# The second batch's normalised rows, turned by way of DRAM and VectorE instead of on TensorE

## The reference

```python
def _layernorm(x, axis=-1, eps=1e-05):
    m = jnp.mean(x, axis=axis, keepdims=True)
    v = jnp.var(x, axis=axis, keepdims=True)
    return (x - m) / jnp.sqrt(v + eps)
...
# attention: x is (2, 512, 512), 32 heads of 16
def proj(w):
    y = jnp.einsum('bsd,ed->bse', x, w)
    return y.reshape(B, S, HEADS, D_K).transpose(0, 2, 1, 3)
q, k, v = (proj(w_q), proj(w_k), proj(w_v))
scores = jnp.einsum('bhqd,bhkd->bhqk', q, k) / jnp.sqrt(jnp.float32(D_K))
attn = jax.nn.softmax(scores, axis=-1)
out = jnp.einsum('bhqk,bhkd->bhqd', attn, v)
...
# ffn: 8 experts, 800 wide, the two best for each token
h1 = jnp.einsum('th,efh->tef', xt, w1)
h3 = jnp.einsum('th,efh->tef', xt, w3)
act = jax.nn.silu(h1) * h3
expert_out = jnp.einsum('tef,ehf->teh', act, w2)
y = jnp.einsum('te,teh->th', w_full, expert_out)
...
x = x + _L0_attn_ref(_layernorm(x, axis=-1), ...)
x = x + _L0_ffn_ref(_layernorm(x, axis=-1), ...)
```

## Time and profile before

| | |
|---|---|
| device time, median of 3 runs | 544.2 us (543.85 to 544.46) |
| the profiled execution: its own time | 544.47 us |
| the profiled execution: span | 542.7 us |
| PE busy | 528.0 us, 97% of the span |
| DVE busy | 386.5 us, 71% |
| ACT busy | 321.2 us, 59% |
| mean granted TensorE clock | 0.994 of full speed |

### The profile page before, as it was taken

One profiled execution on the slowest core, in us unless ns is written; L12 is line 12 of the kernel. 1 busy time (PEld: TensorE's weight loads), 2 busy tenths in 40 slices (PEclk: granted clock), 3 DMA queues, 4 the chain that ended last, 5 costly groups with the idle time before them and its releaser, 6 DMA issues.

```text
span 542.7 us, 10567 instructions
## 1 busy us (share of the span) xinstructions
PE 528.0 (97%) x3925; PEld 388.4 (72%) x3925; DVE 386.5 (71%) x722; ACT 321.2 (59%) x476; POOL 116.9 (22%) x146
## 2 busy tenths in 40 slices
PE   7999999999999999999999999999999999999992
PEld 6887665343333434334868989999999999999991
DVE  6924766999998999943979986836648284666650
ACT  4422115888778788777373465746576575757540
POOL 3400111001020220722001320432342321242112
PEclk9999999999999999999999999999999999999997
DMA  8381267675685470033645698774846757585122
GB/s 298 148 104 14 42 110 84 103 95 79 97 104 74 72 159 15 14 101 99 240 159 170 225 372 266 198 259 111 312 80 220 223 154 269 124 297 162 40 36 38
DMA packets 29743, 78.24 MB, mean 144 GB/s; under 512 B 8572, under 2 KB 9596, under 8 KB 25210
## 3 DMA queue, kind: packets, MB, share of 16 engines
q1 hardware_dynamic: 24394, 68.84, 47.1%
q0 software_dynamic: 5296, 8.69, 8.6%
HBM read 53.11 MB, written 9.32 MB: 115 GB/s over the span
## 4 chain that ended last, share of the span: by engine, by line
PE 89%; DVE 5%; DMA 1%; issue 1%; POOL 1%; ACT 1%; SPq 0%; POOLq 0%; DVEq 0%
PE ps L719 17%; PE ps L721 16%; PE ps L720 16%; PE ps_o L734 12%; PE ps L747 7%; PE ps L759 5%; PE ps_m L747 3%; DVE neg_max L1458 3%; PE ps L787 2%; PE ps_o L719 1%; PE ps_m L1016 1%; DMA x_sb<-x 1%; PE ps L1068 1%; PE ps L1071 1%; PE ps_o L720 1%
## 5 line engine op out<-in xcount | busy, mean ns | idle before, releaser
L1241 ACT ACTIVATE probs_t<-ps 128x1024 f32<-128x1024 f32 x128 | 125.7, 1023 | 28.1 <-PE ps_o L734 23.6
L1458 DVE TENSOR_REDUCE neg_max<-ps 128x1 fp32r<-128x512 f32 x171 | 111.2, 681 | 7.2 <-PE ps L747 4.5
L719 PE MATMUL ps<-xgT_hi,w_hi 128*128 128x256 f32 (+7 forms) x380 | 109.4, 288 | 0.0
L721 PE MATMUL ps<-xgT_hi,w_lo 128*128 128x256 f32 (+7 forms) x380 | 108.6, 286 | 0.0
L720 PE MATMUL ps<-xgT_lo,w_hi 128*128 128x256 f32 (+7 forms) x380 | 108.5, 286 | 0.0
L759 PE MATMUL ps<-q_stack,k_stack 49*128 49x512 f32 x256 | 83.8, 444 | 0.0
L734 PE MATMUL ps_o<-probs_t,v_ones 128*32 128x256 f32 (+1 forms) x944 | 79.6, 409 | 0.1
L719 PEld LDWEIGHTS ps<-xgT_hi,w_hi 128*128 128x128 f32 x380 | 72.0, 189 | 0.3 <-DVE xgT_lo L1733 0.2
L720 PEld LDWEIGHTS ps<-xgT_lo,w_hi 128*128 128x128 f32 x380 | 72.0, 190 | 0.1
L721 PEld LDWEIGHTS ps<-xgT_hi,w_lo 128*128 128x128 f32 x380 | 72.0, 189 | 0.0
L747 PE MATMUL ps<-k_stack,q_stack 48*128 48x512 f32 x171 | 68.6, 458 | 0.5 <-DVE neg_max L1458 0.5
(11 more groups left out here) (326 smaller groups left out, 981.6 us busy)
## 6 DMA issues: line engine op xcount, KB each, us to landing
w_sb<-w SPq DMA_DIRECT2D x16, 1024.0 KB, 7.2
w_sb<-w SPq DMA_DIRECT2D x8, 1536.0 KB
w_sb<-w SPq DMA_DIRECT2D x8, 1152.0 KB, 8.3
q_stack<-q_hi SPq DMA_DIRECT2D x32, 128.0 KB, 4.8
k_stack<-k_hi SPq DMA_DIRECT2D x32, 128.0 KB, 4.6
q_stack<-q_lo SPq DMA_DIRECT2D x16, 128.0 KB, 4.4
k_stack<-k_lo SPq DMA_DIRECT2D x16, 128.0 KB, 5.7
q_hi<-o_raw SPq DMA_DIRECT2D x16, 128.0 KB, 4.8
```

The lines of the kernel that those rows point to most:

```text
L719: pe.matmul(o, x_hi, w_hi, start=start, stop=False)
L721: return pe.matmul(o, x_lo, w_hi, start=False, stop=stop)
L1241: a.activation(probs_t[:, kc % 2, 2 * half:2 * half + 2, :], ps4[:, 2 * (n % 2):2 * (n % 2) + 2, :], ACT.Exp, scale=D ** -0.5).then_inc(s_ ...
L1458: v.tensor_reduce(neg_max[:, g % 2, col:col + 1], max_bank(g, u2), AX.X, ALU.max, negate=True).then_inc(s_mx, 1)
```

## The change

The sixteen transposes of batch 1 leave PE. In their place:

1. SP waits until all 8 tiles are normalised (`s_xn`), writes the four tiles of batch 1 to a DRAM tensor `xn_rows` in one transfer of 1 MB, waits for it (`s_xw`), and reads it back in four transfers of 256 KB. Read n takes columns 128n to 128n+127 of every row to partitions 32n to 32n+31, in pieces of 512 bytes. All five stand in SP's queue ahead of `ready(0)` and `stack(0)`.
2. DVE, at job ("t", 1, 0), waits for the four reads (`s_xr`) and turns the four tiles in 32x32 blocks, in place.
3. ACT and DVE then make `xnT_hi` and `xnT_lo` of batch 1 from `x_sb` in SBUF, with a step of four elements, instead of from PSUM.
4. Block turning puts hidden index 4p + c on partition p in chunk c. So the weights of q, k and v are laid out in this order by the host, in the same sizes, and the transposes of batch 0, which stay on PE, read `x_sb` with a step of four elements.

```diff
+    xn_dram = nc.dram_tensor("xn_rows", [S, HID], f32, kind="Internal").ap()
...
+        s_xw, s_xr, s_xd1 = sem("s_xw"), sem("s_xr"), sem("s_xd1")
...
+        on_pe = [j[:2] != ("t", 1) for j in jobs]
+        j_count = [sum(on_pe[:n + 1]) for n in range(len(jobs))]
...
+        def x_turned(n):
+
+            _, b, i = jobs[n]
+            if b:
+                return x_sb[:, TPB + i, :].rearrange("p (t c) -> p c t", c=HC)
+            return job_bank[n].rearrange("p (c t) -> p c t", c=HC)
...
             sp.dma_start(xn2_dram[0:1, :], rec_row[0:1, :]).then_inc(s_rows, 16)
+
+            sp.wait_ge(s_xn, NT)
+            sp.dma_start(xn_dram[:, :].rearrange("(n p) h -> p n h", p=P), x_sb[:, TPB:NT, :]).then_inc(s_xw, 16)
+            sp.wait_ge(s_xw, 16)
+            pieces = x_sb[:, TPB:NT, :].rearrange("p n (g k) -> p (n g) k", k=P)
+            for n in range(P // BLOCK):
+                sp.dma_start(pieces[BLOCK * n:BLOCK * (n + 1), :, :],
+                             xn_dram[:, n * P:(n + 1) * P].rearrange("(m j) k -> j m k", j=BLOCK)).then_inc(s_xr, 16)
...
-                        last = pe.transpose(o[:, c * P:(c + 1) * P], x_sb[:, b * TPB + i, c * P:(c + 1) * P], ident[:, :])
+                if on_pe[n]:
+                    before = [m for m in range(n) if on_pe[m] and bank_of[m] == bank_of[n]]
...
+                            last = pe.transpose(o[:, c * P:(c + 1) * P],
+                                                x_sb[:, i, :].rearrange("r (p c) -> r c p", c=HC)[:, c, :], ident[:, :])
...
-                a.wait_ge(s_job, n + 1)
+                a.wait_ge(s_job, j_count[n])
                 if kind == "t":
-                    a.activation(xnT_hi[:, :, i * P:(i + 1) * P], o.rearrange("p (c t) -> p c t", c=HC),
-                                 ACT.Copy).then_inc(s_ja, 1)
+                    if not on_pe[n]:
+                        a.wait_ge(s_xd1, i + 1)
+                    a.activation(xnT_hi[:, :, i * P:(i + 1) * P], x_turned(n), ACT.Copy).then_inc(s_ja, 1)
...
                 if kind == "t":
+                    if (b, i) == (1, 0):
+                        v.wait_ge(s_xr, 16 * (P // BLOCK))
+                        for t in range(TPB, NT):
+                            blocks = x_sb[:, t, :].rearrange("p (g k c) -> p g c k", k=BLOCK, c=HC)
+                            v.transpose(blocks, blocks).then_inc(s_xd1, 1)
                     v.wait_ge(s_ja, a_count[n])
                     at = slice(i * P, (i + 1) * P)
-                    v.tensor_tensor(xnT_lo[:, :, at], job_bank[n].rearrange("p (c t) -> p c t", c=HC),
-                                    xnT_hi[:, :, at].bitcast(f32), ALU.subtract).then_inc(s_jd, 1)
+                    v.tensor_tensor(xnT_lo[:, :, at], x_turned(n), xnT_hi[:, :, at].bitcast(f32),
+                                    ALU.subtract).then_inc(s_jd, 1)
...
-        "wq": rows_first(np.asarray(L0_attn_w_q).T[:, order]),
+        "wq": fours_first(np.asarray(L0_attn_w_q).T[:, order]),
```

More of the change, by code:

```diff
@@ L625, in _ @@
                                base=0, pattern=[[1, E], [-1, E]], channel_multiplier=0).then_inc(s_const, 1)
-            pool.wait_ge(s_job, n_of["q", 1, HC - 1] + 1)
+            pool.wait_ge(s_job, j_count[n_of["q", 1, HC - 1]])
             prepare(1)
-            pool.wait_ge(s_job, n_of["k", 1, HC - 1] + 1)
+            pool.wait_ge(s_job, j_count[n_of["k", 1, HC - 1]])
             prepare(2)
-            pool.wait_ge(s_job, len(jobs))
+            pool.wait_ge(s_job, j_count[-1])
             prepare(3)
@@ L806, in _ @@
                     keep_warm(job_bank[NB - 1], 6)
[L807 to L813, removed]
-                        last = pe.transpose(o[:, c * P:(c + 1) * P], x_sb[:, b * TPB + i, c * P:(c + 1) * P], ident[:, :])
[L815 to L820, removed]
-                    else:
[L822 to L828, removed]
-                        else:
-                            last = three(o, *(t[:, at] for t in w2), *x2, c == 0, c == HC - 1)
@@ L831, in _ @@
-                last.then_inc(s_job, 1)
+                if on_pe[n]:
+                    before = [m for m in range(n) if on_pe[m] and bank_of[m] == bank_of[n]]
+                    if before:
+                        job_read(pe, before[-1])
+                    o = job_bank[n]
+                    if kind == "t":
+                        pe.wait_ge(s_xn, b * TPB + i + 1)
+                        for c in range(HC):
+                            last = pe.transpose(o[:, c * P:(c + 1) * P],
+                                                x_sb[:, i, :].rearrange("r (p c) -> r c p", c=HC)[:, c, :], ident[:, :])
+                    else:
+                        which = "qkv".index(kind)
+                        at = slice(i * P, (i + 1) * P)
+                        opening = kind == "q" and (b, i) in ((0, 0), (0, 1), (1, 0))
+                        if opening:
+                            last = opened(o, at, b, i)
+                        else:
+                            pe.wait_ge(s_wl, which + 1)
+                            pe.wait_ge(s_jd, d_count[n_of[("t", b, TPB - 1)]])
+                        for c in range(0 if opening else HC):
+                            x2 = [t[:, c, :] for t in (xnT_hi, xnT_lo)]
+                            w2 = [t[which][:, c, :] for t in (w_hi, w_lo)]
+                            if kind == "v":
+                                last = three(o, *(t[:, at] for t in x2), *w2, c == 0, c == HC - 1)
+                            else:
+                                last = three(o, *(t[:, at] for t in w2), *x2, c == 0, c == HC - 1)
+                    last.then_inc(s_job, 1)
@@ L1227, in _ @@
                 if (s, p) == (0, 1):
-                    a.wait_ge(s_job, len(jobs))
+                    a.wait_ge(s_job, j_count[-1])
                     a.activation(v_ones[:, NT - 1, :, :, 0], ps_o.rearrange("p (h d) -> p h d", d=D),
@@ L1836, in rows_first, with fours_first @@
         return np.ascontiguousarray(w_t.reshape(r // P, P, n).transpose(1, 0, 2).reshape(P, -1))
+    def fours_first(w_t):
+        return np.ascontiguousarray(w_t).reshape(P, -1)
     order = np.array([(8 * c + 4 * half + 2 * p + par) * D + d for c in range(HC)
@@ L1852 @@
         "x": np.asarray(L0_attn_x).reshape(T, HID),
-        "wq": rows_first(np.asarray(L0_attn_w_q).T[:, order]),
-        "wk": rows_first(np.asarray(L0_attn_w_k).T[:, order]),
-        "wv": rows_first(np.asarray(L0_attn_w_v).T),
+        "wq": fours_first(np.asarray(L0_attn_w_q).T[:, order]),
+        "wk": fours_first(np.asarray(L0_attn_w_k).T[:, order]),
+        "wv": fours_first(np.asarray(L0_attn_w_v).T),
         "wo": rows_first(np.asarray(L0_attn_w_o).T),
```

## The result

| | before | changed |
|---|---|---|
| device time, median | 544.12 us | 550.71 us |
| lowest and highest of 6 runs | 543.70 to 544.57 | 549.25 to 552.76 |
| ratio, with its 95% interval | | 1.0121 (1.0104 to 1.0139) |
| the profiled execution: its own time | 544.47 us | 552.76 us |
| the profiled execution: span | 542.7 us | 550.7 us |

The change makes the kernel slower by 6.6 us in the median. One slow run of the first experiment (632.18 us, granted clock 0.75) and one of the eleven of the kernel before beside it (1246.67 us) are left out of the times and ratios.

A forecast was written before the change was run, and what follows sets the result against it. PE, 89% of the chain, was taken to bound the kernel. To the profiled 544.47 us, 4.3 for late stack 0 and 1.2 for the clock gave 550.0, or 549.7 for the median; range 546.6 to 554.6 us.

The forecast's parts named there:

- The slack of 2.3 us: Before PE's first product on stack 0: last transfer lands at 44.1 us, wanted at 46.37; 0.3 us left after the change.
- The write: On SP ahead of stack 0: 1 MB issued at 25.3 us, landing after 5.5 (bounds 4.8 and 6.2), at 30.8.
- The reads at 244 GB/s, 4.3 us: Four reads into 32 partitions each, at twice the 16-partition rate: bytes flow from 31.9 to 36.2 us, bounds 2.6 and 8.6.
- Stack 0 behind them: Stack 0's bytes queue behind the reads, 36.2 to 49.1 us, landing at 50.6; first product at 50.7, costing 4.3 us.
- The clock, 1.2 us: PE idles 6.3 us before the first product on stack 0 and loses 2.4 GHz: 1.2 us, bounds 0 and 3.
- The block transposes, ACT and DVE: hidden: Batch 1's turning (0.69 to 3.2 us a tile), copies and subtractions cost nothing, covered by PE's stall for stack 0.
- The weight loads of batch 0: nothing: Strided loads in batch 0's transposes on PE add 0; a rival put them at twice the time, +2.2 us, chance 0.1.
- the reads hardly hold the stack up: Rival: SP's issues set stack 0's time, +2.6 us, clock may or may not fall: 546.8 to 548 us, chance 0.19.
- they are as slow as stack 0: Rival: the reads flow as slowly as stack 0's transfers, 8.6 us instead of 4.3: 554.0 us, chance 0.17.
- The faster case: Rival: stack 0's last transfer lands within 5.5 us of issue, by 46.3 us; 542.3 us if PE never waits; chance 0.04.
- The PE saving of 1.94 us: Batch 1's transposes leaving PE free 1.94 us before stack 0, but PE only comes to the wait earlier.

The follow-up runs named there:

- the first experiment: The kernel before, with the write and four reads added on SP into a buffer nobody reads then, PE's sixteen transposes kept: 550.5 us, ratio 1.0108.
- the second experiment: The changed kernel without the write and four reads, DVE turning batch 1's rows as they lie: 590.66 us, total not comparable because token loads differ.

## Why the prediction was right

The forecast was 549.7 us in a range of 546.6 to 554.6; it came out at 550.71. Both the side and the mechanism held: stack 0 late behind the write and the reads, PE waiting for it, the clock lost. The sizes are less good than the sum: by the medians the wait cost 4.0 us where the forecast had 4.3, and the clock 2.6 where it had 1.2. Point by point:

- **The slack of 2.3 us, which decides.** Right. In the second experiment PE came 1.6 us earlier, and the first product started 0.14 us behind the stack's landing, so nothing of the slack was left, where the forecast had 0.3.
- **The write.** Forecast: issued at 25.3, landed at 30.8 us. It was issued at 26.45 and landed after 4.4 us, at 30.8. Two errors cancel: DVE ended the normalisation 1.1 us later in this execution (24.51 + 1.92 = 26.4), and the landing was 1.1 us shorter than the 5.5 that I took from a load's row. That the two met at 30.8 is luck. In the seven other traces that have the write on SP it was issued between 24.7 and 25.8 us and landed after 4.4. The 4.4 is under my lower bound of 4.8. The write's last bytes moved at about 30.1 us, as the row of the other write had it; the 1.5 us that I added for the landing, from stack 0's, were 0.7.
- **The reads at 244 GB/s, 4.3 us.** A bit too fast. From 31.9 to 49.4 us the reads and stack 0, 2.62 MB, went through in 17.5 us; at 125 GB/s the stack takes 12.6 of them, which leaves 4.9 us for the reads, 214 GB/s. This is an estimate of their share, not a stretch of their own, since the first bytes of stack 0 ran beside them. The last read landed at 40.3 us, where I had 37.7; in the traces in which the write was issued by 24.9 us and the reads had this order it was 37.0 to 37.4. The Trainium skill ("SBUF — State Buffer", section "Door 1: The DMA port swizzle") states 189 GB/s for 32 partitions and 1 MiB, from which 5.5 us would follow. The trace lies between that and my doubling of the 16-partition rate, 0.6 us from either.
- **Stack 0 behind them.** Forecast: bytes done at 49.1, landed at 50.6, first product at 50.7. They were done at 49.4, landed at 51.34, first product at 51.48. The cost here is 5.1 us, where the forecast had 4.3. The longer reads (0.6 us), less a stack that moved at 125 GB/s and not at 122 (0.3), and a longer landing (1.9 us behind the last bytes, not 1.5) make up these 0.8 us. The 5.1 us hold the late normalisation of this execution: with 44 matmuls, where the write was issued at 24.90, the first product is only 3.7 us late. The opening began 0.7 us earlier in this execution (11.71 to 10.97 us for the first product of q), which made PE's idle time longer, with the later end 7.6 us and not 6.3, and changed nothing at its end.
- **The clock, 1.2 us.** This is the term that was mis-sized: it is 2.8 us in the profiled execution, 2.0 in the first experiment, 2.4 with the round trip on the other queue (58.31 - 52.10 = 6.21 against 3.83), 2.6 by the medians of the change and of the kernel with 44 matmuls. I took the loss from the first matmuls of the span, where PE ran slowly for 2.8 us. Here the clock stayed at 0.50 for 4.5 to 6.8 us of matmuls after the wait, about twice as long. The upper bound of 3 us held. Half of a stretch at 0.50 comes nearer (2.2 to 3.4), but no row of the kernel before showed how long such a stretch is.
- **The block transposes, ACT and DVE: hidden.** Right in the change, and nearer to the lower bound. DVE's four tiles in the changed kernel are one row, answering:

```profile
40.31 4.03 DVE L1518 STREAM_TRANSPOSE x_sb<-x_sb 128x512 f32<-128x512 f32 x4 [5.96 <-DMA x_sb<-xn_rows]
```

  1.0 us a tile, where the bounds were 0.69 and 3.2. DVE was done at 44.3, `xnT_lo` at 48.2, PE asked at 51.5. The kernel with the round trip on GpSimd's queue shows what it costs if that cover is gone: with the rows 7 us later, DVE's work was the bound. The copies and subtractions were 1.1 us each and not the 0.6 to 0.7 that I had, and where stack 0 was on time PE waited 0.3 us for the last copy.
- **The weight loads of batch 0: nothing.** Right in time, for another reason than I had. Line 835 of the changed kernel, answering, and the sixteen in PE's timeline:

```profile
L835 PEld LDWEIGHTS ps<-ident,x_sb x16: 197/209/212, 8.0 to 9.8; 128*128 128x128 f32 x16
```

```profile
8.07 2.08 PE L835 MATMUL ps<-ident,x_sb 128*128 128x128 f32 x16
```

  A strided load takes 209 ns instead of 140, so it is not free, but the sixteen took 2.08 us, where the kernel before took 2.13: the loads lie beside the matmuls. The cacheline note of the Trainium skill ("SBUF — State Buffer", section "Door 1: The DMA port swizzle"), by which a step of four fp32 elements costs nothing, gave the right sum here and not the right duration. My own reason for the nothing, that writes and reads keep their size, says nothing on the loads.
- **The rivals.** That the reads hardly hold the stack up (546.8 to 548) did not happen in the change: 17.5 us went by for both, where the stack alone takes 12.6. But two relatives came near it: the reads into 128 partitions, and the one execution with the other order (548.25 us), where stack 0 landed at 47. That they are as slow as stack 0 (554.0) is ruled out by 214 GB/s. The faster case needed a landing within 5.5 us, and it took 11.2.
- **The PE saving of 1.94 us.** Counted right and worth nothing, as the prediction said. But had stack 0 been on time, I would have claimed 1.9 us, and 0.9 to 1.0 us is what came out in two comparisons, 0.3 of the difference being the wait for ACT's longer copy.

The sum against the profiled execution was 544.47 + 4.3 + 1.2 = 550.0 and is 544.47 + 5.1 + 2.8 = 552.4, with 552.76 measured. Against the median the forecast is nearer than against the execution that it was worked out for: the terms of the profiled one are all at their upper end.

## What to carry to other kernels

- Before work is moved from the bounding engine to a transfer, look at which transfers already stand close to the path there. A slack of 2.3 us on the last landing was worth more than the 1.9 us of work that went, and the price is set by bytes in front of that landing, not by the queue on which they are issued.
- A wait of TensorE can cost twice: the wait, and, in every trace here with 2.9 us of idling or more at this place, another 2.0 to 2.8 us lost to the half clock. If a wait can't be avoided, fill it; if a wait is for many transfers, let the first user ask for the few that it needs.

## What the runs showed of the hardware

- The granted clock fell after an idle time of 3.1 us (reads into 128 partitions) and after 2.9 (reads in another order) as it did after 7.6, and the loss was 2.8 us in all three; after 4.4 us of idling it was 2.0, after 7.8 it was 2.4. The length of the wait does not set the price.
- An ACT copy of 128x512 from SBUF with a step of four elements takes 1.13 us, from PSUM without a step 0.60; these are two rows of line 1227 in the changed kernel, one for each batch:

```profile
L1227 ACT ACTIVATE xnT_hi<-ps x4: 594/600/614, 8.8 to 10.2; 128x512 fp32r<-128x512 f32 x4
L1227 ACT ACTIVATE xnT_hi<-x_sb x4: 1118/1131/1132, 41.5 to 45.5; 128x512 fp32r<-128x512 f32 x4
```

  DVE's subtraction goes from 0.68 to 1.08 us likewise. Step and memory change at once in these, but the same kernel has both operations on operands in SBUF without a step, with twice the elements, in the splitting of the experts' weights (lines 1286 and 1605):

```profile
L1286 ACT ACTIVATE w_hi<-w_sb x48: 1043/1053/1082, 275.6 to 512.8; 128x1024 fp32r<-128x1024 f32 x48
L1605 DVE TENSOR_TENSOR w_lo<-w_sb,w_hi x48: 1207/1218/1270, 284.4 to 515.9; 128x1024 fp32r<-128x1024 f32 x48
```

  1024 elements take ACT 1.05 us there, less than 512 with the step, and DVE 1.22, hardly more. So it is the step that costs and not the memory, as with the weight load, SBUF in both cases, that goes from 140 to 209 ns.
- With transfers under way on two queues both were late (14.9 us to landing for stack 0, up to 14.5 for the reads), where on one queue the reads landed within 8.0 us and stack 0 within 11.2.
- Three products one behind another on the same half of the partitions held PE 0.24 us longer than three that alternate between the halves: 44.53 to 45.42 us in the change with the split wait, 46.37 to 47.03 in the kernel before.
